# Cross-attention stack on one core: an output product, x's last chunks and transposed probabilities change places with scores, sums, norms and exponents

## What is computed

```
def grouped(x, cond, wq, wk, wv, wo, norm_w):
    q = rmsnorm(x, norm_w) @ wq;  k = cond @ wk;  v = cond @ wv
    attn = softmax(einsum('bgrts', q, k) * scale)
    return x + (attn @ v) @ wo
def masked(x, cond, mA, mB, Wq, Wk, Wv, Wo, bo, iA, iB):
    logits = (x @ Wq) @ (cond @ Wk).T * scale + bias_of(mA, mB, iA, iB)
    return softmax(logits) @ (cond @ Wv) @ Wo + bo + x
x = masked(grouped(masked(grouped(x, ...), ...), ...), ...)
```

## Time and profile before

| | |
|---|---|
| median of 3 runs | 1622.84 us (1622.69 to 1625.6) |
| the profiled execution | 1622.62 us |
| its span, first to last instruction | 1620.8 us |
| PE busy | 1576.1 us, 97% |
| DVE, POOL, ACT busy | 67%, 55%, 47% |
| chain that ended last | PE 80%, DVE 13%, issue 4%, DMA, POOL and ACT 1% each |
| granted TensorE clock, mean | 0.996 |

### The profile page before, as it was taken

One profiled execution on the slowest core, in us unless ns is written; L12 is line 12 of the kernel. 1 busy time (PEld: TensorE's weight loads), 2 busy tenths in 40 slices (PEclk: granted clock), 3 DMA queues, 4 the chain that ended last, 5 costly groups with the idle time before them and its releaser, 6 DMA issues.

```text
span 1620.8 us, 22823 instructions
## 1 busy us (share of the span) xinstructions
PE 1576.1 (97%) x8160; PEld 1330.6 (82%) x8160; DVE 1092.8 (67%) x1825; ACT 766.2 (47%) x1353; POOL 885.4 (55%) x809
## 2 busy tenths in 40 slices
PE   8999999999999999999999999999999999999998
PEld 7998987878878887878787887888787888888787
DVE  6677658766676668756876567665865577656764
ACT  4566656334633465335633463345533554255431
POOL 0532356556754676457655575467645765457531
PEclk9999999999999999999999999999999999999999
DMA  9999562122311331122312232133112231222101
GB/s 337 317 327 372 194 225 75 44 65 98 104 59 33 130 111 41 38 92 85 98 46 65 92 111 59 33 130 111 40 39 82 85 101 53 66 92 85 53 1 52
DMA packets 118431, 171.92 MB, mean 106 GB/s; under 512 B 35760, under 2 KB 69040, under 8 KB 112176
## 3 DMA queue, kind: packets, MB, share of 16 engines
q1 hardware_dynamic: 115424, 153.16, 28.9%
q10 hardware_dynamic: 2736, 16.78, 2.6%
q0 software_dynamic: 160, 0.53, 0.1%
HBM read 118.53 MB, written 51.91 MB: 105 GB/s over the span
## 4 chain that ended last, share of the span: by engine, by line
PE 80%; DVE 13%; issue 4%; DMA 1%; POOL 1%; ACT 1%; SPq 0%; DVEq 0%; POOLq 0%; ACTq 0%
PE OB L364 15%; PE OB L366 14%; PE OB L365 14%; PE SB L364 7%; PE SB L366 7%; PE SB L365 7%; PE TB L481 4%; DVE x L1045 2%; PE MX L364 2%; PE MX L366 2%; PE MX L365 2%; DVE pT L916 2%; PE MX L481 2%; DVE small L1019 1%; DVE prob L1015 1%
## 5 line engine op out<-in xcount | busy, mean ns | idle before, releaser
L1240 POOL TENSOR_TENSOR prob<-prob,small 128x512 f32<-128x512 f32 x256 | 277.3, 1087 | 331.1 <-DVE small L1034 331.1
L777 ACT ACTIVATE pT<-TB 128x512 fp32r<-128x512 f32 x192 | 113.7, 592 | 260.2 <-PE TB L481 260.2
L1234 POOL TENSOR_TENSOR prob<-prob,small 128x512 f32<-128x512 f32 x128 | 136.3, 1065 | 160.3 <-DVE small L1009 160.3
L1015 DVE SCALAR_TENSOR_TENSOR prob<-SB,aux 128x512 f32<-128x512 f32 x128 | 87.9, 686 | 185.4 <-PE SB L366 185.4
L364 PE MATMUL OB<-pT,foldN 128*128 128x512 f32 x512 | 205.0, 400 | 1.0 <-DVE pT L916 1.0
L364 PE MATMUL SB<-foldM,xhl 128*128 128x512 f32 x512 | 201.0, 393 | 4.0 <-issue 3.7
L916 DVE TENSOR_TENSOR pT<-TB,pT 128x512 fp32r<-128x512 f32 x192 | 127.1, 662 | 108.6 <-ACT pT L777 108.6
L365 PE MATMUL OB<-pT,foldN 128*128 128x512 f32 x512 | 199.9, 390 | 0.0
L366 PE MATMUL OB<-pT,foldN 128*128 128x512 f32 x512 | 199.9, 390 | 0.0
L366 PE MATMUL SB<-foldM,xhl 128*128 128x512 f32 x512 | 199.7, 390 | 0.0
L365 PE MATMUL SB<-foldM,xhl 128*128 128x512 f32 x512 | 199.4, 389 | 0.0
(11 more groups left out here) (159 smaller groups left out, 4109.6 us busy)
## 6 DMA issues: line engine op xcount, KB each, us to landing
prob<-in_wkvM_dram SPq DMA_DIRECT2D x32, 512.0 KB, 6.6
ring<-s_fm SPq DMA_DIRECT2D x64, 256.0 KB, 5.2
ring<-s_fn SPq DMA_DIRECT2D x64, 256.0 KB, 2.6
out_dram<-x ACTq DMA_DIRECT2D x15, 1024.0 KB, 3.9
s_fm<-prob SPq DMA_DIRECT2D x32, 256.0 KB, 5.1
wraw<-in_wqG_dram SPq DMA_DIRECT2D x8, 1024.0 KB, 8.5
s_fn<-x SPq DMA_DIRECT2D x32, 256.0 KB, 4.9
ring<-in_xT_dram SPq DMA_DIRECT2D x32, 256.0 KB, 3.4
```

The costliest lines, as they stand in the source:

```text
L777: act.activation(pT[:, t % 2, 0, :], t_bank(ph, t)[:, :], ACT.Copy).then_inc(S["pt_hi"], 1)
L1015: dve.scalar_tensor_tensor(out=own, in0=bank, scalar=M_SCALE, in1=row, op0=ALU.mult, op1=ALU.add).then_inc(S["biased"], 1)
L1234: pool.tensor_tensor(own, own, hmax[u % 2].unsqueeze(2).broadcast_to([P, HH, KEYS]), ALU.subtract).then_inc(S["evac"], 1)
L1240: pool.tensor_tensor(own, own, rsum[u % 2].unsqueeze(2).broadcast_to([P, HH, KEYS]), ALU.mult).then_inc(S["normed"], 1)
```

## The change

Only the order of instructions changes; their number and kind do not.

- PE, phase 1 (`grouped_grouped`): the second half of the third output product (`out_part(it, 1, 2, 1)`) moves from before the scores of step 7 to after them and after the first transpose of phase 2.
- PE, tail: the first two transposes of the last output phase move from the start of `grouped_masked(ITS, tail=True)` to before the last scores of the last pair.
- ACT: `x_hi` of chunk 2 (and its square) moves ahead of the last exponent of the pair before.
- DVE, phase 2: `evac(it, 2, 0)`, `pt_lo(it, 2, 2)` and `ot_lo` move ahead of `sums(it, 1, 7)`.
- DVE, phase 3: `pt_lo(it, 3, 1)` moves ahead of `sums(it, 2, 6)` and `sums(it, 2, 7)`.
- POOL, phase 0: `x_lo` of chunks 2 and 3 (and their sums of squares) move ahead of the norms of steps 6 and 7 of the pair before.

```diff
@@ PE
             def grouped_masked(it, tail=False):
                 for u in range(STEPS):
-                    if u % 2 == 0 and (u > 0 or tail):
+                    if u % 2 == 0 and u > 0:
                         transposes(it, 0, u, False, tail)
                         transposes(it, 0, u + 1, False, tail)
@@ PE
             def grouped_grouped(it, first):
                 scores(it, 1, 0, first)
-                for u in range(1, STEPS):
-                    if u + 2 < KC:
-                        transposes(it, 1, u + 2, first)
-                    if u + 1 < KC:
-                        product(it, 1, u + 1, first)
-                    if u == STEPS - 2:
-                        scores(it, 1, u, first)
-                    if u + 1 < KC:
-                        out_part(it, 1, (u - 1) // 2, (u - 1) % 2)
-                    if u != STEPS - 2:
-                        scores(it, 1, u, first)
+                for u in range(1, STEPS - 2):
+                    transposes(it, 1, u + 2, first)
+                    product(it, 1, u + 1, first)
+                    scores(it, 1, u, first)
+                    out_part(it, 1, (u - 1) // 2, (u - 1) % 2)
+                product(it, 1, KC - 1, first)
+                scores(it, 1, STEPS - 2, first)
+                scores(it, 1, STEPS - 1, first)
                 transposes(it, 2, 0, first)
+                out_part(it, 1, 2, 1)
                 out_part(it, 1, 3, 0)
                 out_part(it, 1, 3, 1)
@@ PE, masked_masked
                 product(it, 3, KC - 1, first)
+                if it == ITS - 1:
+                    transposes(ITS, 0, 0, False, True)
+                    transposes(ITS, 0, 1, False, True)
                 scores(it, 3, STEPS - 1, first)
@@ ACT, body
                     exp(it - 1, 3, STEPS - 2)
+                x_hi(it, 0, 2, first)
+                if not first:
                     exp(it - 1, 3, STEPS - 1)
-                x_hi(it, 0, 2, first)
                 x_hi(it, 0, 3, first)
@@ DVE, body
                 sums(it, 1, STEPS - 2, first)
+                evac(it, 2, 0, first)
+                pt_lo(it, 2, 2)
+                ot_lo(2 * it + 1, 0)
                 sums(it, 1, STEPS - 1, first)
-                for s in range(1, STEPS):
-                    if s > 1:
+                for s in range(2, STEPS):
+                    if s > 2:
                         pt_lo(it, 2, s)
-                    if s % 2 == 0:
+                    if s > 2 and s % 2 == 0:
                         ot_lo(2 * it + 1, s // 2 - 1)
                     evac(it, 2, s - 1, first)
-                    if s >= 2:
-                        sums(it, 2, s - 2, first)
+                    sums(it, 2, s - 2, first)
...
                 xb_lo(it, 2)
+                pt_lo(it, 3, 1)
                 sums(it, 2, STEPS - 2, first)
                 sums(it, 2, STEPS - 1, first)
-                pt_lo(it, 3, 1)
@@ POOL, body
                     norm(it - 1, 3, STEPS - 3)
+                x_lo(it, 0, 2, first)
+                x_lo(it, 0, 3, first)
+                if not first:
                     norm(it - 1, 3, STEPS - 2)
                     norm(it - 1, 3, STEPS - 1)
-                x_lo(it, 0, 2, first)
-                x_lo(it, 0, 3, first)
                 inverse(it, 0)
```

## The result

| | before | changed kernel |
|---|---|---|
| median | 1623.26 us (4 runs) | 1576.51 us (4 runs, 1576.0 to 1577.25) |
| the profiled execution | 1622.62 | 1576.36 |
| its span | 1620.8 | 1574.6 |
| granted TensorE clock, mean | 0.996 | 1.00 |

The ratio is 0.971, with a 95% interval of 0.9698 to 0.9722. Forecast were 1584.0 and a range from 1578 to 1592.

The account below looks back on a forecast made before the run. PE's instruction stream plus its standing time was taken to bound the kernel. Gains of 15.0 + 6.4 + 11.8 + 4.4 + 1.0 + 0 = 38.6 us took 1622.62 to 1584.0 us, range 1578 to 1592.

Parts of the forecast that it names:

- Part 1: Phase 0, pairs 1 to 7: moving x_lo and x_hi earlier removes PE's wait before chunk 2; gain 15.0 us.
- Part 2: Pairs 3, 4, 6, 7: the x_lo gap provokes four half-clock stretches, which vanish with it; gain 6.4 us.
- Part 3: Phase 2, eight times: evac(2,0) and pt_lo(2,2) ahead of sums(1,7) remove PE's wait before t=3's transposes; gain 11.8 us.
- Part 4: Phase 3, eight times: pt_lo(3,1) ahead of two sums removes PE's wait before the transposes into MX; gain 4.4 us.
- part 5: Before the last output phase: earlier transposes remove DVE's idle time ahead of a pt_lo; gain 1.0 us.
- part 6: Phase 1: scores ahead of output products leave xnew and the wait before phase 2's first scores unchanged; gain 0.
- thin cover: Phase 2: after the next, longer subtraction, pt_lo(2,3) ends at 983.0 against PE's need at 983.2 us.
- part 6 does remove the wait: Rival: phase 1's new order removes the wait before phase 2's first scores, 5.7 us more gain; 1578.3 us, chance 0.05.
- half-clock rival: Rival: the clock stretches stay at another place, not being the x_lo gap's doing; 1590.4 us, chance 0.10.
- phase 2 keeps a part: Rival: phase 2 keeps part of its wait before transposes, 0.5 us per pair; 1588 us, chance 0.09.
- that of phase 0: Rival: in phase 0 x_lo(2) is still last, so that wait and the clock stretches stay; 1605.4 us, chance 0.04.
- the slower one: Rival: late part_lo(4) delays a ring slot's reload in phase 2; slower than before if reload exceeds 9.7 us; chance 0.02.

Follow-up runs that it names:

- x_only: Kernel before with only x_hi(2) moved ahead of the last exponent on ACT and x_lo(2), x_lo(3) ahead of two norms on POOL; 1600.17 us, ratio 0.9861.
- evac_only: Kernel before with only evac(2,0), pt_lo(2,2) and ot_lo moved ahead of sums(1,7) on DVE in phase 2; 1608.08 us, ratio 0.9909.
- pt_only: Kernel before with only pt_lo(3,1) moved ahead of two sums on DVE in phase 3; 1616.57 us, ratio 0.9959.
- tail_only: Kernel before with only two transposes of the last output phase moved ahead of the last scores on PE; 1621.77 us, ratio 0.9995.
- all_but_p6: Changed kernel with phase 1's old order on PE put back; 1583.67 us, ratio 0.9753 to before.
- p6_last_only: Kernel before with only out_part(2,1) moved behind the last scores and phase 2's first transpose, loop order kept; 1621.61 us, ratio 0.9992.
- x_norm6_ahead: Kernel before with x_hi(2) and x_lo moved as in the change, but the norm of step 6 kept ahead of x_lo(2); 1609.13 us, ratio 0.9913.

## Why the prediction was wrong, point by point

| part | forecast | measured | from |
|---|---|---|---|
| 1, x_lo and x_hi | 15.0 | 15.5 (7 × 2.22) | period of x_only |
| 2, clock | 6.4 | 6.4 (4 stretches gone) | profiles |
| 3, evac and pt_lo, phase 2 | 11.8 | 11.5 (8 × 1.44) | period of evac_only |
| 4, pt_lo, phase 3 | 4.4 | 4.2 (8 × 0.52) | period of pt_only |
| 5, tail | 1.0 | 1.0 | trace of tail_only |
| 6, phase 1 | 0 | 6.4 | spans of all_but_p6 and the changed kernel |

Parts 3 and 4 are the gain of a period times eight. In pair 0 itself the traces show 0.96 and 0.21, but its length also differs by up to 0.7 us between kernels whose edit doesn't touch it.

**The step that failed is part 6.** Without it the changed kernel's span is 1581.0, 39.8 us below that of before, where the other five parts were forecast at 38.6. Part 6 adds 6.4, most of the 7.6 by which the 46.2 of the spans exceed the forecast; of the other 1.2 half is the prologue, which ended at 159.8 instead of 160.3. It failed in two ways.

First I misread the edit. The text says that the new order puts "the last scores and the first transpose of phase 2 one `out_part`" earlier. That is only the second half, and the list of changes ahead of the diff names no more; the diff itself also changes the loop, from output product before scores to scores before output product in steps 1 to 5. The old loop hides this in its conditions: `scores` stands once under `u == STEPS - 2` before `out_part` and once under `u != STEPS - 2` behind it. For the edit that I described, 0 was right: p6_last_only has 0.13 us per period, 1 us in all.

Second, "DVE's order is unchanged and it is busy throughout, so `xnew` stays" is true only of work whose inputs do not move. Each busy stretch begins with a wait for something, and this one began with the copy of step 5's scores. With the scores of step 5 one output product earlier, `evac(1,5)` starts 4.5 us ahead of output product (3,0) instead of 3.0, and the work behind it slides forward until a new wait of 0.54 us for `ot_lo`'s input holds it. With step 7's copy earlier too, `xnew` starts 0.79 us sooner and the wait before phase 2's scores is gone. The bound I gave for this, 5.7 us, was nearly right for its size (the wait before phase 2's scores, eight times), but I gave it a chance of 0.05 and argued against it with that very row. The lower end of the range, 1578, rested on this bound. The profiled 1576.36 lies 1.9 below the 1578.3 of that rival: 0.7 since part 6 gives 6.4 and not 5.7 (pair 0 gains 1.4 by it, the others 0.7), and 1.2 from outside part 6, as above.

**What held.** Part 1 to half a microsecond, with its spare time (0.45 against 0.4). Part 2's cause, which the four gap widths show. Part 3 with its restart loss, its moved collision, its thin cover and the hidden ring wait. Part 4, part 5. The change of period was forecast as 175.2 to 171.1; all_but_p6 has 171.05.

The rival that came true is "part 6 does remove the wait". The half-clock rival, the "phase 2 keeps a part" rival, that of phase 0 and the slower one did not happen. The Trainium skill's rule on the port pair (SBUF — State Buffer, SBUF: two separate sides), that one engine blocks the other for a whole instruction, agrees with the pair 0.69 and 1.60 above: the stretched subtraction ran 954.72 to 956.32, behind a `part_lo` from 954.49 to 955.77. It ends 0.55 us after that `part_lo`, as the one of 1.79 us did in before (978.47 against 977.92); so the stretched time is the rest of POOL's operation plus 0.55, not plus 0.69 as the prediction has it.

## What to carry to other kernels

When the end of a busy stretch matters, find what released its first instruction, and ask whether the edit moves that; "this engine has no idle time here" bounds nothing if the whole stretch can slide. Where two chains end within a few hundredths of a microsecond of each other, moving either gains almost nothing (here 0.12 and 0.13 us a pair) and moving both gains the whole (0.77): test an edit's halves before you call one of them useless. And unroll a loop by hand on both sides of a diff, step by step, before pricing it.

## What the runs showed of the hardware

A gap in TensorE's stream can cost more than its width. In pairs 1 to 7 of the traces, 27 of the 56 gaps of 2.08 us were followed by a stretch of 3.4 us at granted clock 0.50 that cost 1.6 us; after 2.66 us 6 of 7; after 1.1 us and less none. Cutting the gap to half, without closing it, already gave back the clock: x_norm6_ahead keeps 1.1 us of the gap in each of seven pairs and gains 13.5 us, of which 7.1 are the gap's own width.
